# Inverse roots of the norms: Sqrt on ScalarE replaced by a guess from the bits and Newton steps on GpSimd

## What is computed

```python
def _ln(x, g, b):                                   # layer 0, three times: g1/be1, g2/be2, gf/bf
    m = x.mean(-1, keepdims=True)
    v = ((x - m) ** 2).mean(-1, keepdims=True)
    return (x - m) * jax.lax.rsqrt(v + EPS) * g + b
...
def rmsnorm(x, w):                                  # layer 1
    var = jnp.mean(x * x, axis=-1, keepdims=True)
    return x * jax.lax.rsqrt(var + EPS_NORM) * w
...
x = queries + out                                   # layer 2
mu = jnp.mean(x, axis=-1, keepdims=True)
var = jnp.mean(jnp.square(x - mu), axis=-1, keepdims=True)
return (x - mu) * jax.lax.rsqrt(var + LN_EPS) * gamma + beta
...
normed = hidden_states * jax.lax.rsqrt(var + EPS) * norm_w   # layer 3
```

## Time and profile before

| | us |
|---|---|
| median of 3 runs | 2273.82 (2262.84 to 2274.65) |
| the profiled execution | 2284.93 |
| its span, first to last instruction | 2283.2 |
| TensorE busy in it | 2050.4 |
| VectorE / ScalarE / GpSimd busy | 1382.6 / 1145.8 / 744.6 |
| mean granted TensorE clock | 0.956 of full |

### The profile page before, as it was taken

One profiled execution on the slowest core, in us unless ns is written; L12 is line 12 of the kernel. 1 busy time (PEld: TensorE's weight loads), 2 busy tenths in 40 slices (PEclk: granted clock), 3 DMA queues, 4 the chain that ended last, 5 costly groups with the idle time before them and its releaser, 6 DMA issues. The chain is left out here.

```text
span 2283.2 us, 38499 instructions
## 1 busy us (share of the span) xinstructions
PE 2050.4 (90%) x14610; PEld 1351.3 (59%) x14610; DVE 1382.6 (61%) x3055; ACT 1145.8 (50%) x1755; POOL 744.6 (33%) x914
## 2 busy tenths in 40 slices
PE   4999999999998879998899898998999996989999
PEld 2333433333343368876565565665677775988989
DVE  5866776676678366636435454452677783756654
ACT  2356465555645756533526445263555554545444
POOL 3023123124113243322616336153110101646646
PEclk8799999999999999998989999999999997999999
DMA  7606305403520000036622707220422210000000
GB/s 153 128 17 115 43 6 90 80 1 72 89 59 1 1 15 1 10 91 95 133 39 54 121 7 136 51 66 5 167 84 92 77 41 1 9 11 13 15 12 20
DMA packets 77773, 126.67 MB, mean 55 GB/s; under 512 B 16650, under 2 KB 34826, under 8 KB 77582
## 3 DMA queue, kind: packets, MB, share of 16 engines
q1 hardware_dynamic: 74966, 122.63, 25.7%
q10 hardware_dynamic: 2624, 1.58, 0.2%
HBM read 93.59 MB, written 30.32 MB: 54 GB/s over the span
## 5 line engine op out<-in xcount | busy, mean ns | idle before, releaser
L1068 DVE TENSOR_REDUCE nmx_causal<-banks 128x1 f32<-128x333 f32 (+4 forms) x896 | 435.4, 538 | 173.2 <-PE banks L799 171.3
L957 ACT ACTIVATE probs_causal<-banks 128x1024 f32<-128x1024 f32 (+5 forms) x384 | 330.6, 899 | 263.4 <-PE banks L824 259.6
L799 PE MATMUL banks<-ks_causal,qs_causal 96*128 96x333 bf16 (+4 forms) x896 | 272.1, 340 | 13.8 <-DVE nmx_causal L1068 7.8
L722 POOL TENSOR_SCALAR_AFFINE_SELECT probs_window<-probs_window 128x512 f32<-128x512 f32 (+1 forms) x272 | 161.7, 601 | 289.9 <-ACT probs_window L957 279.0
L722 POOL TENSOR_SCALAR_AFFINE_SELECT probs_causal<-probs_causal 128x512 f32<-128x512 f32 (+2 forms) x160 | 92.5, 579 | 458.9 <-ACT probs_causal L957 458.5
L824 PE MATMUL banks<-qs_causal,ks_causal 97*128 97x512 bf16 (+5 forms) x896 | 210.1, 330 | 17.9 <-ACT probs_causal L957 13.9
L1068 DVE TENSOR_REDUCE nmx_window<-banks 128x2 f32<-128x384 f32 (+2 forms) x320 | 141.0, 460 | 106.1 <-PE banks L799 103.5
L848 PE MATMUL banks<-probs_causal,v_causal 128*17 128x512 f32 (+5 forms) x1792 | 186.2, 489 | 0.0
L957 ACT ACTIVATE probs_window<-banks 128x768 f32<-128x768 f32 (+2 forms) x128 | 99.7, 785 | 110.8 <-PE banks L824 110.5
L797 PEld LDWEIGHTS banks<-below,identb 128*128 128x128 bf16 x512 | 49.6, 98 | 173.5 <-DVE nmx_causal L1068 124.8
L799 PEld LDWEIGHTS banks<-ks_causal,qs_causal 96*128 96x128 bf16 x896 | 86.6, 100 | 103.0 <-DVE nmx_causal L1068 59.1
(11 more groups left out here) (256 smaller groups left out, 4164.0 us busy)
## 6 DMA issues: line engine op xcount, KB each, us to landing
fs_masked<-in_fside SPq DMA_DIRECT2D x32, 616.0 KB, 3.7
ks_causal<-zk SPq DMA_DIRECT2D x96, 137.6 KB
ks_window<-zk SPq DMA_DIRECT2D x96, 137.6 KB
qs_causal<-zq SPq DMA_DIRECT2D x96, 128.0 KB
qs_window<-zq SPq DMA_DIRECT2D x96, 128.0 KB
zk<-parts_causal SPq DMA_DIRECT2D x24, 275.2 KB, 2.8
zk<-parts_window SPq DMA_DIRECT2D x24, 275.2 KB, 2.4
zq<-parts_causal SPq DMA_DIRECT2D x24, 256.0 KB, 7.3
```

Source lines behind the costliest of these rows:

```text
L722: pool.affine_select(out=v, in_=v, compare_op=ALU.is_ge, fill=0.0, base=const, pattern=[[0, QH], [by_c, wd]], channel_multiplier=by_p).the ...
L799: ins = pe.matmul(bk[:, c:c + m], qs[q][0:KR, h, t * P:(t + 1) * P], ks[q][0:KR, h, key:key + m], start=cover is None, stop=True, skip_gro ...
L957: ins = act.activation(dst, src, ACT.Exp, scale=DH ** -0.5)
L1068: dve.tensor_reduce(dst, src, AX.X, ALU.max, negate=True).then_inc(emptied_v, 1)
```

## The change

Every `root` token moves from ScalarE to GpSimd, at the same place of the order. VectorE, after variance + eps, writes a first value of the inverse root into row 1: the bits of the number taken as an integer, times -0.5, plus a constant, and taken as a float again (`guess_root`). GpSimd (`root_of`) makes three Newton steps of four operations on 128x8 from it, each of the twelve waiting for the one before by a semaphore of its own, `newton`; the last writes row 2 and tells VectorE. VectorE's reciprocal is left out. The folded layer keeps its Sqrt.

```diff
@@ take_spread
     if centred:
-        dve.tensor_scalar(sd[:, 0, :], mv[:, :, 1], eps, None, ALU.add).then_inc(sem("spread"), 1)
+        chain(dve.tensor_scalar(sd[:, 0, :], mv[:, :, 1], eps, None, ALU.add))
     else:
         chain(dve.tensor_tensor(sd[:, 1, :], mv[:, :, 0], mv[:, :, 0], ALU.mult))
         chain(dve.tensor_tensor(sd[:, 2, :], sd[:, 1, :], mv[:, :, 1], ALU.add))
-        dve.tensor_scalar(sd[:, 0, :], sd[:, 2, :], eps, None, ALU.add).then_inc(sem("spread"), 1)
+        chain(dve.tensor_scalar(sd[:, 0, :], sd[:, 2, :], eps, None, ALU.add))
+    guess_root(dve, sd).then_inc(sem("spread"), 1)
@@ normalise_tiles
     if 0 in tiles:
         dve.wait_ge(sem("root"), time + 1)
-        chain(dve.reciprocal(sd[:, 2, :], sd[:, 1, :]))
@@
-def root_of(act, sem, sd, time=0):
-    act.wait_ge(sem("spread"), time + 1)
-    act.activation(sd[:, 1, :], sd[:, 0, :], ACT.Sqrt).then_inc(sem("root"), 1)
+def guess_root(dve, sd):
+
+    return dve.tensor_scalar(sd[:, 1, :].bitcast(I32), sd[:, 0, :].bitcast(I32), -0.5, HALF_BITS, ALU.mult, ALU.add)
+
+
+def root_of(pool, sem, sd, step, time=0):
+
+    pool.wait_ge(sem("spread"), time + 1)
+    v, y, t = sd[:, 0, :], sd[:, 1, :], sd[:, 2, :]
+    for last in (False, False, True):
+        step(pool.tensor_tensor(t, y, y, ALU.mult))
+        step(pool.tensor_tensor(t, t, v, ALU.mult))
+        step(pool.tensor_scalar(t, t, -0.5, 1.5, ALU.mult, ALU.add))
+        if last:
+            pool.tensor_tensor(t, t, y, ALU.mult).then_inc(sem("root"), 1)
+        else:
+            step(pool.tensor_tensor(y, t, y, ALU.mult))
@@ masked_schedule
-        act.append((end + 0.05, ("root", b)))
+        pool.append((end + 0.05, ("root", b)))
```

More of the change, by code:

```diff
@@ L339, in products @@
     return ins
+I32 = mybir.dt.int32
+HALF_BITS = 1597463007.0
 class Chain:
@@ L649, in gpsimd @@
     def gpsimd(pool):
+        newton = Chain(pool, sem("newton"))
         def begin():
@@ L697, in step @@
                 pool.tensor_copy(pad[:, 1, :, S:P], xnT[:, :, 0:P - S]).then_inc(padded, 1)
-            if what == "middle" or what == "rest" and args[0]:
+            if what == "root":
+                root_of(pool, sem, sd, newton, args[0])
+            elif what == "middle" or what == "rest" and args[0]:
                 b, u, half = args
@@ L889, in step @@
                 bk = ring.bank(token)
-            if what == "root":
-                root_of(act, sem, sd, args[0])
-            elif what == "shift":
+            if what == "shift":
                 b, q = args
@@ L1153, in gpsimd @@
     def gpsimd(pool):
+        newton = Chain(pool, sem("newton"))
         def step(token):
             what, *args = token
-            if what == "norm" and args[1] == 0:
+            if what == "root":
+                b, time = args
+                root_of(pool, sem, sd[time], newton, 2 * b + time)
+            elif what == "norm" and args[1] == 0:
                 b, _, i = args
@@ L1207, in step @@
             what, *args = token
-            if what == "root":
-                b, time = args
-                root_of(act, sem, sd[time], 2 * b + time)
-            elif what in ("turn", "up"):
+            if what in ("turn", "up"):
                 place = ring if what == "turn" else own_banks
@@ L1666, in _ @@
                         .then_inc(sem(what + "_ready"), 1)
+                elif what == "root":
+                    root_of(pool, sem, sd[:, b % 2], newton, b)
                 elif what == "bias":
@@ L1773, in _ @@
                 what, b, *args = token
-                if what == "root":
-                    act.wait_ge(sem("spread"), b + 1)
-                    act.activation(sd[:, b % 2, 1, :], sd[:, b % 2, 0, :], ACT.Sqrt).then_inc(sem("root"), 1)
-                    continue
                 if what == "lower":
@@ L1856, in _ @@
                     dve.wait_ge(sem("moments"), NT * (b + 1))
-                    dve.tensor_scalar(sd[:, b % 2, 0, :], mv[:, b % 2, :, 1], 1e-5, None, ALU.add)\
-                       .then_inc(sem("spread"), 1)
+                    chain(dve.tensor_scalar(sd[:, b % 2, 0, :], mv[:, b % 2, :, 1], 1e-5, None, ALU.add))
+                    guess_root(dve, sd[:, b % 2]).then_inc(sem("spread"), 1)
                     continue
@@ L1863, in _ @@
                         dve.wait_ge(sem("root"), b + 1)
-                        chain(dve.reciprocal(sd[:, b % 2, 2, :], sd[:, b % 2, 1, :]))
                     dve.scalar_tensor_tensor(x[:, b, i, :], x[:, b, i, :], mv[:, b % 2, i, 0:1], gamma[:], ALU.subtract,
```

## The result

The changed kernel takes 2294.12 us (median of 4 runs, 2291.22 to 2301.16), the kernel before in the same session 2268.33 (2259.7 to 2274.65). The ratio is 1.0116, with a 95% interval of 1.0084 to 1.0148: 26 us slower, 19 to 34. It lies inside the range on record, 2264 to 2306. But I gave 0.50 to no change that can be told, 0.42 to slower, and forecast +10.4 us. The sign of the sum was right and its size was not: 16 us are missing from it. That the range held is luck in part: its upper end was there for rival (b), a dear step, and the steps turned out cheap.

The account below looks back on a forecast made before the run. TensorE, busy 90% of the span, was taken as the bound, so edits count by its waits. Ten terms summed to +10.4 us, 0.46% on the profiled 2284.93; applied to the runs' median 2273.82 this gave 2284.2, range 2264 to 2306.

Parts of the forecast that it names:

- rival (b): GpSimd's roots: a step is dear, 5.5 us a root instead of 3.25; +41.9 us in all, 2315.5; chance 0.20.
- Prices: GpSimd's twelve-step root: 0.27 us a step, 3.25 a root; ScalarE loses two loads and a Sqrt, 2.81 us, at a root.
- Term 5: Feed-forward batches 1 to 3: normalisations start earlier, TensorE's waits of 1.38 and 0.52 go; -5.2 us together.
- s + 3.7: Any root: first normalisation starts 3.7 us after s, the start of the spread's last old instruction, if no GpSimd mask interferes.
- terms 3 to 5: Feed-forward: batch 0 first norm +2.0, its second norm -2.8, batches 1 to 3 -5.2 us.
- Term 6: Window batch 0's root, in feed-forward's end: +0.6 us.
- Term 7: Window batches 1 to 3: TensorE waits for the late normalised tiles, 2.3 us each; +6.9 us.
- Terms 1 to 4 and 8 to 10: Start +2.5, causal +2.7, feed-forward batch 0 +2.0 and -2.8, masked batches 0-2 -0.6, masked batch 3 +3.0, folded +1.3 us.
- Terms 9 and 10: Masked batch 3, root with nothing beside it, +3.0 us; folded layer, a table load before its Sqrt, +1.3 us.
- signs that I had set: Window roots: TensorE's tile wait grows from 1.2 to 3 us or more; forecast wrong if window layer isn't 5 longer.
- Rival (a): TensorE's later waits absorb VectorE's late normalisations, ScalarE's stalls were the price; -5.4 or -9.1 us; chance 0.20.
- Rival (c): Nothing moves: loads and roots lie under TensorE's work nearly everywhere; 2280.6 us; chance 0.55 shared with the forecast.

Follow-up runs that it names:

- e2: All-VectorE Newton root of e1, plus twelve GpSimd steps behind each spread that nobody reads; ratio 1.0118 to the kernel before.
- e12: Changed kernel with the eight feed-forward roots put back to ScalarE's square root and VectorE's reciprocal; ratio 1.0112 to the kernel before.
- e7: Changed kernel with statistics, spread and root of batches 1 to 3 of both attention layers 12 places earlier; ratio 1.0027 to the kernel before.
- e5: Changed kernel with two Newton rounds (8 steps) instead of three; ratio 1.0015 to the kernel before.
- e6: Changed kernel with six Newton rounds (24 steps) instead of three; ratio 1.0436 to the kernel before.
- e1: Changed kernel with the three Newton rounds as nine operations on VectorE instead of twelve on GpSimd; ratio 1.0116 to the kernel before.
- e3: e1 with ScalarE's square root and its table loads put back, into a tile that nobody reads; ratio 1.0218 to the kernel before.
- e9: Changed kernel with e5's and e7's edits together: two Newton rounds and earlier attention statistics; ratio 0.9964 to the kernel before.

## Why the prediction was wrong in size, by its own steps

**Prices: right.** Twelve steps take 3.3 us, start 0.28 apart and last 0.20 each (forecast 3.25, 0.27, 0.21). From the guess to the normalisation it is 3.6 to 3.7 where nothing interferes (forecast 3.5). Rival (b), the dear step, did not come in: 14 of the 20 roots take 3.3 us, and six, all between 810 and 962, take 3.7 to 4.7, with one to three steps held. Two steps in a row are held at the first root of feed-forward batch 1 (timeline of the changed kernel):

```profile
810.16 1.30 DVE L1303 TENSOR_TENSOR hT<-full,hT 128x512 fp32r<-128x512 f32 x2
810.33 0.58 POOL L401 TENSOR_TENSOR sd_ff<-sd_ff 128x8 f32<-128x8 f32 x1 [3.66 <-DVE sd_ff L393]
...
810.99 0.53 POOL L402 TENSOR_TENSOR sd_ff<-sd_ff 128x8 f32<-128x8 f32 x1
...
811.60 0.20 POOL L403 TENSOR_SCALAR sd_ff<-sd_ff 128x8 f32<-128x8 f32 x1
```

0.58 and 0.53 instead of 0.20 while VectorE takes two Gelu remainders, each with two inputs in SBUF. By the Trainium skill, "SBUF — State Buffer", section "Who interferes with whom", this is the shared port, and it stood in the prediction as a rule that would stretch these roots alone. The trace agrees in kind: five of feed-forward's roots and window batch 0's, which lies among them, have steps of 0.53 to 0.70 us, and the window's other roots have none. In sum this is 4.8 us of GpSimd's time; what it costs the kernel no run shows, since nobody waits for the steps of e2.

**Term 5 failed, and is the largest miss: -5.2 forecast, about 0 measured.** The step that failed is "in batches 2 and 3 they would start some 4 us earlier than now", and with it that both of TensorE's waits would go. The first normalisations of batches 2 and 3 start 5.64 us behind their variance instead of 7.78, so 2.1 earlier and not 4: three steps of their root are held, and it takes 4.7 instead of 3.3. TensorE's wait of 1.38 went. The second ones start 1.0 later, not earlier (5.53 instead of 4.51), and there the 0.52 grew fourfold. I took ScalarE away from VectorE's wait and forgot that the wait has a second end, the root itself. By my own rule of s + 3.7 a second root would have been 0.8 earlier. Nearly all of the 1.8 us in between are the add and the guess beside the bias additions (0.7), the additions in front of the root (0.5) and the held first step (0.45). I had named the additions, but only for coming late themselves. e12's traces agree: even, where terms 3 to 5 gave the layer a gain of 6.

**Term 6 and the clock are the rest of the +4.1 in that stretch.** Window batch 0's root costs 2.6 (forecast 0.6), 1.1 by the wait and 1.5 by a lower clock behind it; another 1.5 is clock behind batch 3's turn, for which the sum had no term.

**Term 7: the cause was right, the path in part, the size half.** The late normalisation is 2.4 us by its own rows and was forecast at 2.3. But I had TensorE waiting for the tiles longer, and that wait stayed (1.22 before, 0.88, 1.23 and 1.23 now): it waits for the maxima behind the normalisation. It measured +5.0, +4.0 and +5.4 (+3.4, +5.5 and +3.9 against the first trace of the kernel before). The sum priced a pause of TensorE at its length, and left out what the clock did behind it: 8 us at 0.57. The trace of before had it at some of its own pauses, so the term could have been bounded. e7 takes most of both away and gets back 13.4 in these stretches.

**Terms 1 to 4 and 8 to 10, as far as they can be told apart, were right within 1.4 us.** Terms 9 and 10 give 4.4 for 4.3, and TensorE's waits bear them out one by one: 10.41 to 13.28 us at the last masked root's barrier and 2.46 to 3.91 in the folded layer, so 2.87 and 1.45 for a forecast of 3.0 and 1.3. In the causal layer, 4.1 for 2.7, one trace cannot tell the two numbers apart.

**Two of the signs that I had set point the wrong way.** TensorE's wait for the normalised tiles at the window's roots did not grow, which I had called a sign of (a); it was another of its waits that grew. And the window layer as a whole (965 to 1600) is only 1.7 us longer in the traces, where less than 5 was to mean that the forecast is wrong. Its three roots cost 14.4 and the clock elsewhere gave 12.7 back, so a whole layer of one execution was too coarse a sign.

**Rival (a) fell.** It said that TensorE makes up for a late normalisation in later waits. e5 and e6 show that on average none of it is made up, from 8 to 24 steps a root. What did pay for itself is feed-forward, where the freed ScalarE gives back about what the roots cost. Rival (c) fell with it: it ended at +6.8, and the interval starts at 19.

**What the forecast would have needed** is one view beside the terms: VectorE's 6.7 us of waiting for roots against up to 3.7 for each of 20. The measured 44.1 are 37 us of new idle time on an engine that TensorE waits for, and a freed ScalarE gives part back. I went root by root, and each time found a reason why part of it was covered.

What is open: why e1's causal layer costs 6 us more than the changed kernel's (e2, with the same code on VectorE, has 3 more, so half of it may be the execution); a kernel with VectorE's root in feed-forward alone and GpSimd's elsewhere was not run. Nor was the price of the freed ScalarE measured by itself, since e3's signal came late.

## What to carry to other kernels

A wait of an in-order engine has to be priced at what stands behind it, and taking one cause out of it only shows the next: ask what ends the wait then, with the releasing engine's own queue in front. A chain of small dependent steps that an in-order engine waits for cost its full length here, on average over 20 uses, unless the order left it time; statistics that came a few rows earlier were worth nearly as much here as a third of the chain taken out. Price a longer pause of TensorE by the granted clock behind it too, not by its length alone.

## What the runs showed of the hardware

- GpSimd: a 128x8 operation takes 0.20 us, and a chain in which each waits for the last starts them 0.28 apart; beside VectorE's Gelu remainders single ones take 0.53 to 0.70. VectorE's take 0.17, 0.20 apart, and 0.49 when one meets a mask of GpSimd.
- A table load of 1.28 us has the next activation 0.02 us behind it (1929.19 + 1.28, then 1930.49 in the rows above), so a switch costs the load and hardly more where ScalarE has work queued.
- TensorE's granted clock after a pause, at the window's roots 1 to 3: with gaps of 3.1 and 0.9 to 1.2 us close together it was 0.50 to 0.56 in the lowest 4 us and stayed down for some 8 us, at all three; with 1.1 alone (e9, all three) it stayed at full speed; with 0.51 and 1.22 (the kernel before) it fell at three places of six, so the same pauses can cost something or nothing.
- The two profiled executions of the kernel before differ by 11.5 us with nothing changed, at mean clocks of 0.956 and 0.964. A comparison of two traces shows places, and only the timed runs show the sum.
